# A new table of turns for two interleaved half passes on PE, ScalarE and VectorE (four layers, one core)

## What is computed

```python
# layer 0: causal attention, 16 heads of 8
a = softmax(where(causal, q @ k.T / sqrt(8), -1e9)); x += (a @ v) @ WO.T
# layer 0 ffn: capacity MoE: 8 experts, top 2, at most int(256/8*1.25) tokens each, 128 -> 512 -> 128
# layer 1: causal attention again; ffn: rmsnorm, attention with shared keys (4 heads),
#          then rmsnorm, router (8 experts, top 2), silu(x @ w1.T) * (x @ w3.T) @ w2.T, and a shared expert
# layer 2: linear attention; ffn: rmsnorm, causal attention (16 heads), rmsnorm,
#          silu(x @ up.T) @ down.T * sum(top 2 gates)
# layer 3: q, k normed to the unit sphere per head; d = arccos(q @ k.T); weight = a power of the distance;
#          out = weights / sum @ v
# layer 3 ffn: three blocks of: linear (quantised weight + LoRA), layernorm, gelu, linear, + residual
```

## Time and profile before

| | us |
|---|---|
| median of 3 runs | 3342.96 (3331.83 to 3349.52) |
| span of the profiled execution, first to last instruction | 3337.4 |
| PE busy | 2641.8 |
| VectorE busy | 1763.9 |
| ScalarE busy | 1912.7 |
| granted clock of TensorE, mean | 0.795 of full speed |

### The profile page before, as it was taken

One profiled execution on the slowest core, in us unless ns is written; L12 is line 12 of the kernel. 1 busy time (PEld: TensorE's weight loads), 2 busy tenths in 40 slices (PEclk: granted clock), 3 DMA queues, 4 the chain that ended last, 5 costly groups with the idle time before them and its releaser, 6 DMA issues.

```text
span 3337.4 us, 46425 instructions
## 1 busy us (share of the span) xinstructions
PE 2641.8 (79%) x18736; PEld 1529.0 (46%) x18736; DVE 1763.9 (53%) x2698; ACT 1912.7 (57%) x1960; POOL 3.6 (0%) x12
## 2 busy tenths in 40 slices
PE   8999999777997789877898688986889868897215
PEld 4666456343563435534355344553445534453102
DVE  5463574545656355553555545654455544563524
ACT  2433435875358753586445864468534685447994
POOL 0000000000000000000000000000000000000000
PEclk7997989659896588966899668986779867987557
DMA  3000000000000000000000000000000000000000
GB/s 128 2 1 1 20 1 1 1 1 8 1 1 1 1 8 1 1 1 0 8 1 1 1 0 8 2 1 1 0 5 2 1 1 0 4 1 1 0 0 6
DMA packets 4561, 18.68 MB, mean 6 GB/s; under 512 B 608, under 2 KB 864, under 8 KB 3808
## 3 DMA queue, kind: packets, MB, share of 16 engines
q1 hardware_dynamic: 4320, 15.38, 1.2%
HBM read 13.28 MB, written 2.10 MB: 5 GB/s over the span
## 4 chain that ended last, share of the span: by engine, by line
PE 54%; ACT 19%; DVE 15%; issue 12%; DVEq 0%; DMA 0%; ACTq 0%; SPq 0%
ACT back_cosines L1320 6%; PE one_ps L1164 2%; PE two_ps L1275 2%; PE one_ps L862 2%; PE two_ps L910 2%; ACT back_cosines L1322 2%; PE one_ps L1710 2%; DVE back_nsum L1330 2%; PE one_ps L1717 2%; ACT L1320 2%; PE one_ps L766 1%; PE one_ps L1723 1%; DVE back_cosines L1393 1%; ACT L1862 1%; PE two_ps L862 1%
## 5 line engine op out<-in xcount | busy, mean ns | idle before, releaser
L1320 ACT ACTIVATE back_cosines<-back_cosines 128x2048 f32<-128x2048 f32 x256 | 472.2, 1899 | 0.5
L933 ACT ACTIVATE front_scratch<-one_ps 128x1152 f32<-128x1152 f32 x168 | 171.5, 1021 | 225.0 <-PE one_ps L848 224.8
L1322 ACT ACTIVATE back_cosines<-back_cosines,wts 128x2048 f32<-128x2048 f32 x128 | 252.4, 1994 | 41.1 <-DVE back_cosines L1393 40.9
L1330 DVE TENSOR_REDUCE back_nsum<-back_cosines 128x8 f32<-128x2048 f32 x64 | 144.4, 2281 | 234.0 <-ACT back_cosines L1320 234.0
L797 DVE TENSOR_REDUCE front_negm<-one_ps 128x8 f32<-128x1024 f32 (+1 forms) x168 | 204.4, 1220 | 56.6 <-PE one_ps L772 55.5
L837 PE MATMUL one_ps<-ident_bf,mask_q 128*128 128x256 bf16 x480 | 93.3, 302 | 80.5 <-ACT front_scratch L933 69.3
L696 ACT ACTIVATE back_cosines<-two_ps,wts 128x512 fp32r<-128x512 f32 x28 | 19.3, 688 | 224.1 <-PE two_ps L910 224.1
L766 PE MATMUL one_ps<-front_qkr 32*128 32x128 f32 (+1 forms) x896 | 136.5, 414 | 14.1 <-issue 8.9
L1393 DVE TENSOR_SCALAR back_cosines<-two_ps 128x2048 f32<-128x2048 f32 x56 | 128.2, 2290 | 28.5 <-PE two_ps L1257 28.3
L933 ACT ACTIVATE back_cosines<-two_ps 128x1152 f32<-128x1152 f32 (+1 forms) x84 | 86.0, 1024 | 92.0 <-PE two_ps L848 92.0
L766 PEld LDWEIGHTS one_ps<-front_qkr 32*128 32x128 f32 x896 | 96.6, 274 | 88.5 <-DVE front_negm L797 46.3
(11 more groups left out here) (630 smaller groups left out, 5795.1 us busy)
## 6 DMA issues: line engine op xcount, KB each, us to landing
wts<-w_dram SPq DMA_DIRECT2D x1, 4184.0 KB, 15.3
front_xin<-x_dram SPq DMA_DIRECT2D x8, 256.0 KB, 4.2
out_dram<-back_z SPq DMA_DIRECT2D x8, 256.0 KB, 2.1
wts<-w_dram SPq DMA_DIRECT2D x1, 1736.5 KB, 19.1
wts<-w_dram SPq DMA_DIRECT2D x1, 1199.0 KB, 5.3
wts<-w_dram SPq DMA_DIRECT2D x1, 1152.0 KB, 16.5
wts<-w_dram SPq DMA_DIRECT2D x3, 256.0 KB, 5.8
wts<-w_dram SPq DMA_DIRECT2D x1, 516.5 KB, 4.8
```

What stands on the lines that cost most here:

```text
L933: nc.scalar.activation(h.probs[:, e % 2, 0:n * HEADW].rearrange("p (k c) -> p k c", c=HEADW), h.ps[:, 0:n, 0:HEADW], ACT.Exp, scale=float( ...
L1320: nc.scalar.activation(cosines, cosines, func, scale=scale).then_inc(h.arc_pass.sem, 1)
L1322: nc.scalar.activation(cosines, cosines, func, scale=scale, bias=C(bias)).then_inc(h.arc_pass.sem, 1)
L1330: nc.vector.tensor_reduce(h.nsum[:, kt, :].rearrange("p (g2 j) -> p j g2", g2=2), h.cosines[:, u % 2, kt * 4 * TOK:(kt + 1) * 4 * TOK].rea ...
```

## The change

Only the numbers in the three tables are new, for all three engines and all three sections. The number of steps of each half in each table is the same. The instructions of one half on one engine stand in the same order as before, with the same waits; their places among those of the other half are new. SP's and POOL's programs are the same. The number of ACT_TABLE_LOADs follows from the new neighbours: in the program's order there are 7, 22 an iteration, and 29 in the three sections before, and 7, 24 and 36 now.

```diff
 ACT_RUNS = {
...
     "both": (
-        1, 3, 2, 2, 2, 4, 3, 1, 1, 1, 2, 9, 4, 4, 2, 3, 2, 1, 2, 2, 12, 2, 2, 4, 3, 4, 2, 2, 3, 2, 2, 8, 1, 2,
...
+        1, 3, 1, 2, 2, 2, 1, 2, 3, 1, 1, 1, 1, 4, 1, 4, 2, 3, 2, 3, 2, 2, 2, 1, 1, 2, 12, 1, 1, 1, 1, 2, 1, 4,
...
```

## The result

Before, the median was 3339.53 us (4 runs, 3331.83 to 3349.52); the changed kernel's is 3394.97 us (4 runs, 3377.52 to 3403.09). The ratio is 1.0149, 95% interval 1.011 to 1.0187: about 50 us slower (37 to 62).

A forecast was written before the change was run, and what follows sets the result against it. It saw PE-bound stretches, two kinds of ScalarE-bound stretches and latency chains at the halves' ends. Loop +10, opening 0 and last section +1 gave +11 on 3342.96, about 3354 us; range 3312 to 3394.

The forecast's parts named there:

- Table loads: Whole kernel: 19 more loads on ScalarE at 1.283 us each without a drain, 24.4 us of ScalarE.
- Loop, +10: Six loop iterations, each put at +1.7 us, +10 in all; bounds about -4 and +8 an iteration.
- (a): Iteration start: the back's projection copies go ahead of the front's last norm step, which waits for PE: +0.9 us.
- (b): Linear attention beside the front's max part: the back's pieces go first, taking back PE's wait: -1.5 us an iteration.
- (c): Second half of arccos: front's first exp goes ahead of two Ln passes, arccos passes move back: +3.9 us an iteration.
- (e): End of the ScalarE-full arccos stretch: front's last mqa exp goes ahead of two Exp passes: -3.7 us an iteration.
- (f): Experts beside qlora blocks: Silu before Gelu -2.1, one load +1.3, back's later residual add +1.6: +0.8 us an iteration.
- Opening, 0: Front halves of the first passes: PE busy 92%, equal loads, one half's gain is the other's loss: 0, bounds ±5 us.
- Last section, +1: Two back halves: later arccos start +13, shorter arccos stretch -6, staggered blocks -6: +1 us, bounds -10 and +19.
- Rival 1: Slower: displaced passes and loads paid in each iteration's ScalarE-full arccos stretch, +45 loop, +5 last section: 3393 us; chance 0.32.
- Rival 2: Faster: the moves help the front, the loop's longer work; loop -25, last section -7: 3311 us; chance 0.26.
- Rival 3: Nothing: whole kernel only shuffled within slack, loads fall into waits: 3343 us; counted with the forecast, together 0.42.

The follow-up runs named there:

- the run of the loop's late part: Kernel before, with each loop iteration in the changed order only after the front half ends moe0: 3345.60 us, ratio 1.0016.
- the early part: Kernel before, with each loop iteration in the changed order until the front half ends moe0, then the order of before: 3376.22 us, ratio 1.0111.
- the run of the last section alone: Kernel before, with the changed order only in the last section (two back halves), opening and loop as before: 3350.02 us, ratio 1.0024.
- the four openings: Traced openings of the kernel before, the changed kernel, changed order in the opening alone, and changed order only after moe0: 333.8, 365.5, 363.3, 389.1 us.

## Why the prediction was right or wrong

The range ended at 3394; by the ratio (1.0149 times the 3342.96 it started from) the time is 3393, by the bare median it is 3395, so it lies at the very end. The point (3354) had the right sign and no more: it gave the most to "no change", and its likeliest sum, +11, was a fifth of the 50. By its steps:

- **Table loads.** The count (19), the price (1.28 us, no drain) and that they are paid where ScalarE is full: right, by the run of 18 added loads. The sign "ScalarE busy about 1937 us" was 7 us too high (1929.8), though the loads themselves took the 24.4 us. The added loads explain at most 12 x 1.28 = 15 us of the loop; and the run of the loop's late part, which holds all twelve, came to +5 (-2 to +12), while the early part, with no load more, came to +37. So the forecast's main term does not carry the loop's loss.
- **Loop, +10.** Measured +16 (9 to 23): right in sign and size, but the terms were not. Starts behind the loop's last L1854, in the timelines of PE, of an iteration of before and one of the run with the changed loop (both 409 to 413 us long):

| start on PE | before | changed loop |
|---|---|---|
| front's norm ahead of moe0 (L557) | 114.4 | 117.3 |
| front's norm ahead of causal1 | 182.2 | 187.0 |
| front's norm ahead of mqa | 282.0 | 278.1 |
| router of moe1 (L1406) | 353.0 | 353.2 |
| end of the iteration | 409.2 | 413.1 |

  Terms (a) and (b), put at -0.6, cost 2.9 by the norm ahead of moe0, and 1.9 more come by causal1, where no term stood. In (c), the front's exps ahead of the arccos passes, put at +3.9, the front's attention wins 8.7 us (from 182.2 to 282.0 against 187.0 to 278.1), and then loses 4.1 in the ScalarE-full stretch behind it. (e), -3.7, is there as a wait (8.79 for 11.44), 2.7 us. (f), +0.8, was up to 3.7. That the sum came near is in part luck.
- **Opening, 0.** This step failed, and by the runs of one section each it is the largest (+37, of which the trace puts 29.5 into the opening, beside +16 and +8). The reason given, that PE is busy at 92% and what one half gains the other loses, takes PE's busy time as fixed. It is not: the same 2596 products took 27 us more, all of it at the lower level, against bounds of -5 and +5 for the section. The forecast's last sentence had named this as what no term held. A hint was there: the earlier trace rows has the clock at 0.90 in the opening, and in the trace of before the two long stretches at the lower level are the first max parts of both halves (40 to 70 us) and the second half's mqa (309 to 347 us).
- **Last section, +1.** The first arccos pass was put at +13 (5 to 22) and came at +33 to +45 in three traces. The direction was right, the size was not. Six groups of PE work were counted at 10 us, and the work ahead of the first Ln grew by 14 to 15. For what the mlps hide less, 3 us were taken; PE's idle time grew by 12. Not counted was the lower level, 7 us in the run of the last section alone and 19 in the changed kernel, where the clock is 0.57 from 2908 to 2948 us (linear attention of both halves) and 0.50 from 3008 to 3028 (the younger half's max part beside the older's attention). Arccos, -6: measured -7 to -8. Tail, -6: measured -11 in the changed kernel, and only -3.5 with the order of the blocks alone. The whole section, put at +1, came to +8 (2 to 14) alone. Blocks of 12 to 13 us for one half: right (Gelus of one half at 3368.25 and 3381.16, 12.9 us).
- **Rivals.** Rival 1 had the time (3393) but not the place. Its deciding sign, a wait ahead of L1104 that stays above 10 us, did not come (8.8 to 9.0). That the measured time lies at its 3393 is luck: it put +45 into the loop and 0 into the opening. Rival 2 fell: the front did gain, as it said, in the attention beside arccos, but not at the end of the iteration. Rival 3 fell.

What stays open: why PE's level falls at one moment and not at another in the same stream. In the opening the traces show what PE did there (products of few columns or on 32 partitions, few long products between), and that is all that is claimed. The neighbours alone do not decide it: the younger half's max part beside the older's attention ran at 0.84 to 1.00 before and at 0.50 in the run of the loop's early part. And that keeping the halves apart would have avoided it is argued from the four openings, not shown by an order that does it better than before.

## What to carry to other kernels

When two instruction streams are merged on a full TensorE, look for the stages at which the granted clock is at its lower level, and ask of a new order which stages it lays beside each other: the same products cost nearly twice the time there (1.87 and 3.62 us). Counts of instructions and of table loads did not show it; windows of the clock did. Part a stretch's loss into work, idle time and lower level before naming a cause: in the opening it was nearly all the lower level, at the start of the last section mostly the other two. And take the sum of such a kernel from several executions, for a single trace can be off by 20 us with the same instructions.

## What the runs showed of the hardware that was not expected

- The same last section, in the same order on every engine, took 475 us in five traces of the table (474.8 to 475.3), 480.8 in one and 494.1 in two. In the slowest, PE's idle time up to the first Ln is that of before (25.3 and 25.5 us) and its busy time 20 us more; full windows hold 110 to 124 instructions of PE at 0.84 to 1.00, and about 75 at 0.50.
- Iterations of the same order within one run are from 406.2 to 416.4 us long.
- Up to the second L1104, PE's busy time runs from 304 to 347 us over the traces of the table. With the part at the lower level counted half it is 266 to 271 us in all that have the same 2596 products.
- 32 products of 128x128 by 512 columns, put between the small ones of mqa, did not raise the granted clock in the traced execution; each took 0.61 us and left it at 0.50.
- A table load of the set that is already loaded costs the same 1283 ns as a switch.
